# First maxima of a causal attention taken inside the feature loop; squares moved from GpSimd to ScalarE

## The reference

```python
q = split(x @ Wq); k = split(x @ Wk); v = split(x @ Wv)          # 16 heads of 16
q_amp = _amp_norm(q)      # a = softplus(t); a / sqrt(mean(a * a) + 1e-6), per head
k_amp = _amp_norm(k)
q_phi = pi * tanh(split(x @ Wqp)); k_phi = pi * tanh(split(x @ Wkp))
scores_dot = einsum(q, k) * scale
scores_phase = (einsum(q_amp*cos(q_phi), k_amp*cos(k_phi)) + einsum(q_amp*sin(q_phi), k_amp*sin(k_phi))) * scale
scores = scores_dot + lam * scores_phase
attn = softmax(where(causal, scores, -inf)); out = einsum(attn, v)
```

## Time and profile before

| | us |
|---|---|
| median of 3 runs | 1952.91 (1946.81 to 1959.45) |
| profiled execution, its time | 1948.98 |
| its span in the profile | 1947.3 |
| TensorE busy | 1737.1 (89% of the span) |
| DVE busy | 1262.3 (65%) |
| ACT busy | 882.6 (45%) |
| granted TensorE clock, mean | 0.941 |

### The profile page before, as it was taken

How to read it: one execution, slowest core, us unless ns; L and a number is a source line. 1 busy time by engine, 2 the same in 40 slices (tenths; PEclk the granted TensorE clock), 3 DMA queues, 4 the chain that set the end, 5 groups by cost and what they waited for, 6 DMA issues and landing times.

```text
span 1947.3 us, 28314 instructions
## 1 busy us (share of the span) xinstructions
PE 1737.1 (89%) x9130; PEld 920.4 (47%) x9131; DVE 1262.3 (65%) x2992; ACT 882.6 (45%) x1035; POOL 366.4 (19%) x478
## 2 busy tenths in 40 slices
PE   6998479999999999999999999977639999999965
PEld 3444234444444444444444444426525666666644
DVE  3677867777777777777777777516525555555536
ACT  2677524455555555555455554544311221221236
POOL 0111211111121111211211112103572111111111
PEclk9999768899999999999999999997759999999988
DMA  3366434011021020110201103016521111111144
GB/s 102 137 238 236 179 129 147 7 36 70 8 73 39 15 90 7 57 50 7 99 12 39 67 7 121 13 60 204 205 95 38 47 43 48 44 43 49 44 132 151
DMA packets 99497, 155.30 MB, mean 80 GB/s; under 512 B 10752, under 2 KB 60736, under 8 KB 99008
## 3 DMA queue, kind: packets, MB, share of 16 engines
q1 hardware_dynamic: 84928, 122.53, 18.9%
q0 software_dynamic: 14464, 31.40, 4.6%
HBM read 87.90 MB, written 65.35 MB: 79 GB/s over the span
## 4 chain that ended last, share of the span: by engine, by line
PE 70%; DVE 8%; ACT 7%; issue 6%; DMA 5%; POOL 2%; SPq 1%; another core or an unknown queue 0%; ACTq 0%; DVEq 0%; POOLq 0%
PE att_ps_s L884 22%; PE exp_ps_h L1564 13%; PE att_ps_o L903 12%; PE att_ps_m L862 10%; PE exp_ps_y L1582 6%; ACT att_probs L931 3%; DMA out_parts<-att_out_t 2%; PE pre_ps_q L311 2%; PE exp_ps_t L1572 2%; PE pre_ps_h L311 1%; DVE att_maxima L945 1%; DMA k_parts<-pre_waves 1%; PE exp_ps_x L1553 1%; POOL sorted_rows L1449 1%; DMA route_a_inv<-inv_rows 1%
## 5 line engine op out<-in xcount | busy, mean ns | idle before, releaser
L931 ACT ACTIVATE att_probs<-att_ps_s 128x1024 f32<-128x1024 f32 (+3 forms) x640 | 563.7, 895 | 484.4 <-PE att_ps_s L884 476.5
L884 PE MATMUL att_ps_s<-att_queries,att_keys 49*128 49x512 f32 (+3 forms) x2560 | 632.8, 561 | 20.9 <-ACT att_probs L931 11.4
L945 DVE TENSOR_REDUCE att_maxima<-att_ps_m 128x1 f32<-128x512 f32 x768 | 487.1, 684 | 153.6 <-PE att_ps_m L862 148.6
L862 PE MATMUL att_ps_m<-att_keys,att_queries 48*128 48x512 f32 (+3 forms) x1280 | 506.5, 605 | 24.1 <-DVE att_maxima L948 15.9
L862 PEld LDWEIGHTS att_ps_m<-att_keys,att_queries 48*128 48x128 f32 x1280 | 197.7, 193 | 315.8 <-DVE att_maxima L945 141.4
L884 PEld LDWEIGHTS att_ps_s<-att_queries,att_keys 49*128 49x128 f32 x2560 | 242.9, 191 | 127.3 <-ACT att_probs L931 85.4
L948 DVE CUSTOM_DVE_ANT_0 att_ps_m<-att_ps_m,att_future 128x128 f32<-128x128 f32 (+3 forms) x512 | 240.3, 514 | 73.4 <-PE att_ps_m L862 72.1
L903 PE MATMUL att_ps_o<-att_probs,att_values 128*32 128x512 f32 (+3 forms) x2560 | 269.3, 535 | 11.1 <-POOL att_probs L1034 11.1
L1564 PE MATMUL exp_ps_h<-keep_w,exp_rows_t 128*128 x568 | 257.4, 596 | 5.5 <-DVE exp_rows_t L1598 5.5
L1640 ACT ACTIVATE exp_hidden<-exp_product 128x512 f32<-128x512 f32 x71 | 44.8, 632 | 343.7 <-DVE exp_product L1623 343.7
L1034 POOL TENSOR_SCALAR_AFFINE_SELECT att_probs<-att_probs 128x512 f32<-128x512 f32 x128 | 81.1, 634 | 491.3 <-ACT att_probs L931 491.2
(11 more groups left out here) (179 smaller groups left out, 1458.6 us busy)
## 6 DMA issues: line engine op xcount, KB each, us to landing
att_queries<-q_parts SPq DMA_DIRECT2D x64, 192.0 KB
att_keys<-k_parts SPq DMA_DIRECT2D x64, 192.0 KB
exp_rows<-sorted_rows SPq DMA_DIRECT2D x71, 129.0 KB, 2.3
v_rows<-pre_v_sb SPq DMA_DIRECT2D x8, 1024.0 KB, 7.1
q_parts<-pre_waves SPq DMA_DIRECT2D x16, 512.0 KB, 4.2
k_parts<-pre_waves SPq DMA_DIRECT2D x16, 512.0 KB, 5.8
att_values<-v_rows SPq DMA_DIRECT2D x32, 256.0 KB
out_parts<-att_out_t POOLq DMA_DIRECT2D x32, 256.0 KB, 6.0
```

The lines of the kernel that those rows point to most:

```text
L862: pe.matmul(take()[:, 0:width], queries[g % 2][half, c, r, P * q:P * q + P], keys[g % 2][half, k, r, 0:width], start=True, stop=True).then ...
L884: mm = pe.matmul(score_tile(unit, first, last)[:, e], keys[g % 2][half, k // TPC, r, P * (k % TPC):P * (k % TPC) + P].bitcast(F32), querie ...
L931: act.activation(probs[:, step % PROBS, DUO * r:DUO * r + DUO, first:last], score_tile(unit, first, last), ACT.Exp, scale=SCALE).then_inc( ...
L945: dve.tensor_reduce(to, buf[:, 0:width], AX.X, ALU.max).then_inc(s_mr, 1)
```

## The change

Four things change.

1. The first 32 groups of maximum tiles of the first quad (64 tiles: chunk 0, chunk 1, and the first 8 of chunk 2's 24 groups) leave the attention. TensorE sends them inside the projections of chunks 4 to 7 (iterations 5 to 8), one group of two tiles after each half of a projection, so 8 groups an iteration; DVE takes them at 8 places of its iteration. They use a ring of two banks, so a send waits until DVE has read the tile two before.
2. The two banks come from `ps_n`, which is gone: `sum_norm` of Q now writes `ps_q`, and waits for the copy of the same iteration's K out of it (`s_qk`).
3. `square` is an ACT activation with lag 2, behind the tanh of Q, where it was a POOL multiplication with lag 1. On DVE the cosine `features` now stand ahead of the copy of K, where they stood behind it. TensorE's loop is written out.
4. The plan starts with 32 groups done and DVE and ACT busy until 8000 ns (`TAIL`). The ones under the second quad's keys are written by SP and no longer by POOL.

```diff
+EARLY_CHUNKS = range(NCH // 2, NCH)
+EARLY_TURNS = 8
+EARLY_GROUPS = len(EARLY_CHUNKS) * EARLY_TURNS
+    def send_early(self, pe):
+        for _ in range(DUO):
+            tile, self.sent = self.sent, self.sent + 1
+            if tile >= len(self.ring):
+                pe.wait_ge(self.s_mr, tile - len(self.ring) + 1)
+            self.send(pe, self.ring[tile % len(self.ring)], *self.early[tile])
...
-        ps_n = n.ps("ps_n", [P, 2, CH])
...
+            def project(i, weight, out, p, ready):
                 for c in range(2):
                     for k in range(DK):
                         mm = pe.matmul(...)
-                return mm
+                    if c == 1:
+                        mm.then_inc(ready, 1)
+                    if i in EARLY_CHUNKS:
+                        maxima.send_early(pe)
...
                 if side == Q:
                     pe.wait_ge(s_sq, i + 1)
+                    pe.wait_ge(s_qk, min(2 * i + 4, 2 * NCH))
...
+            def square(i, p):
+                act.wait_ge(s_amp, i + 1)
+                if since(i, 1):
+                    act.wait_ge(s_norm, 2 * i)
+                act.activation(amp_sq[:, :], amp[:, p], ACT.Square).then_inc(s_sq, 1)
...
             pipelined(act, NCH, [
                 (lambda i, p: phases(i, p, Q), 1),
+                (square, 2),
                 (lambda i, p: norm_exp(i, p) if i < NCH - 1 else None, 3),
...
             pipelined(dve, NCH, [
+                (take_early, 1),
                 (lambda i, p: keep_qk(i, p, Q), 1),
+                (take_early, 1),
                 (abs_phase, 2),
+                (take_early, 1),
                 (norm_amplitudes, 3),
+                (take_early, 1),
+                (lambda i, p: features(i, p, 0), 3),
+                (take_early, 1),
                 (lambda i, p: keep_qk(i, p, K), 1),
-                (lambda i, p: features(i, p, 0), 3),
+                (take_early, 1),
+                (take_early, 1),
+                (take_early, 1),
                 (keep_v, 1),
                 (amplitudes, 1),
                 (keep_x, 0),
                 (lambda i, p: features(i, p, 1), 3)])
...
-            def square(i, p):
-                pool.wait_ge(s_amp, i + 1)
-                if since(i, 1):
-                    pool.wait_ge(s_norm, 2 * i)
-                pool.tensor_tensor(amp_sq[:, :], amp[:, p], amp[:, p], ALU.mult).then_inc(s_sq, 1)
...
-        self.free = dict(pe=0, dve=0, act=0, pool=0)
+        self.free = dict(pe=0, dve=TAIL, act=TAIL, pool=0)
+        self.group = EARLY_GROUPS
```

More of the change, by code:

```diff
@@ L164, in absolute @@
     return dve.tensor_scalar(out.bitcast(U32), in_.bitcast(U32), 0x7FFFFFFF, None, ALU.bitwise_and)
-def prepare(nc, block, small, x, Wq, Wk, Wv, Wqp, Wkp, lambda_raw, q_parts, k_parts, v_rows, first_quad):
+BLOCKS = [TPC * (c + 1) for c in range(QC)]
+FIRST = [sum(BLOCKS[:c]) for c in range(QC)]
+STEPS = sum(BLOCKS)
+QUADS = B * NQ
+CHUNKS = QUADS * QC
+QUAD_LOADS = 16 * (2 * DUO + 1)
+MAX_TILES = [DUO * DUO * TPC * (c + 1) for c in range(QC)]
+SLOTS_PS = 3
+SLOTS_S = 2
+PROBS = 6
+BATCH = 2
+AHEAD = 3
@@ new lines, with chunk_of, own_block, hidden_columns @@
+SUMS = QUAD * CH // P
+SWITCH, SEEN, PLACED, SETTLED, EAGER, TAIL = 200, 200, 2200, 6000, 300, 8000
+def chunk_of(s):
+    return max(c for c in range(QC) if FIRST[c] <= s)
+def own_block(s):
+    c = chunk_of(s)
+    return s - FIRST[c] - TPC * c
+def hidden_columns(s):
+    return P * max(0, own_block(s))
+def ends_chunk(s):
+    return s + 1 in FIRST[1:] + [STEPS]
+def units_of(s):
+    return [(r, hidden_columns(s), CH) for r in range(DUO)]
+UNITS = [(s, *unit) for s in range(STEPS) for unit in units_of(s)]
@@ L321, in project_qk @@
                     pe.wait_ge(s_qk, 2 * i + side)
-                project(side, ps_q, p).then_inc(s_qkp, 1)
+                if side == Q and since(i, 2):
+                    pe.wait_ge(s_ln, 2 * i - 3)
+                project(i, side, ps_q, p, s_qkp)
             def project_phase(i, p, side):
@@ L364, in _ @@
                 (lambda i, p: sum_norm(i, p, K), 2),
-                (turn, 0)])
+                (turn, 0)], unrolled=True)
         @block.scalar
@@ L814, in attend, with put_ones @@
         vacated = {"max": s_mr, "turn_max": s_row}
-        CONSTS = 1
-        LOADS = 16 * (2 * DUO + 1)
+        def put_ones(eng, i):
+            eng.wait_ge(s_made, 1)
+            for e in range(DUO):
+                row = HALF * e + FEAT
+                eng.dma_start(keys[i][row:row + 1].rearrange("p c r t -> p (c r t)").bitcast(F32),
+                              ones[0:QC * DUO * CH // (P // 2)]).then_inc(s_one[i], 16)
         def chunk_row(g, c):
@@ L913, in _ @@
                 elif event == "max":
-                    max_tile(*what)
+                    highest.send(pe, take(), *what)
                 elif event == "turn_max":
@@ L977, in invert @@
                 dve.reciprocal(inverse[:, n % 2], sums[:, n % 2]).then_inc(s_inv, 1)
-            tile = 0
+            tile = DUO * EARLY_GROUPS
             for event, *what in plan:
                 if event == "max":
-                    take_max(*what, tile, ps_m[slots.pop(0)[0]])
+                    highest.take(dve, ps_m[slots.pop(0)[0]], tile, *what)
                     tile += 1
-                    if tile == sum(MAX_TILES[m % QC] for m in range(what[0] + 1)):
-                        negate(what[0], tile)
                 elif event == "turn_max":
```

187 lines of the change are left out of this document (90 added, 97 removed).

## The result

The changed kernel takes **1967.6 us** (median of 11 runs, 1961.5 to 1973.79) against 1952.91 (11 runs, 1946.81 to 1959.76): a ratio of **1.0069**, 95% interval 1.0049 to 1.0089. It is 0.7% slower, which is inside the 1% that the prediction called no change, and the interval lies wholly above 1.

The account below looks back on a forecast made before the run. The loop was taken to be bound by a ring through TensorE, ACT and DVE, the early attention by TensorE's waits and low clock. 8.8 + 46.6 + 2 - 45.5 = +12 gave 1965 us on the median; range 1934 to 1992.

Parts of the forecast that it names:

- case (a): The forecast itself: loop +57, attention -45 us; -5 to +28 with the bounds; chance 0.55.
- The ring: Loop's circle through TensorE, ACT and DVE: square and cosine features lengthen 23.9 to 28.3 us; iterations 3 and 4 +8.8.
- The lockstep: Iterations 5 to 8: sends and takes wait for each other through two banks; 36.1 us each, +46.6 in all.
- The tail: Loop's end: the last square on ACT waits behind `make_waves` and delays the path to the last features, +2 us.
- The start of the attention: Last features to first scores: 6.0 us instead of 14.64, the row being turned already, -8.6.
- To chunk 3: First scores to those of chunk 3: 82 us against 115.7, clock over 0.9, -33.8.
- the -3: At chunk 3's first scores: the slow start of a unit after a wait goes, an estimated -3 us.
- own bound of -12: Attention's smallest gain: only the 64 tiles' own 0.2 us each, all stalls come back; forecast -45.5.
- (b): Rival, loop: the lockstep isn't paid, only square and features lengthen the ring; -19, 1934 us; chance 0.16.
- (c): Rival, attention: stalls come back, scores wait for placed rows or maxima, only some 15 us gained; 1996 us; chance 0.12.
- (d): Rival, loop: TensorE stays at the lower clock from send 5 to V, +5 us an iteration; 1985 us; chance 0.17.
- Part 1: Loop's ring: square and features lengthen it by 4.4 us; DVE's 2.5 us back from POOL's contention don't show.

Follow-up runs that it names:

- e4: The changed kernel with V's projection ahead of the norm's sum of Q on TensorE: 1964.21 us, ratio 1.0067 to the kernel before.
- e1: The changed kernel with DVE's cosine features behind the eighth take, no longer ahead of K's copy: 1960.62 us, ratio 1.0042 to the kernel before.
- e5: The changed kernel with ACT's square ahead of the tanh of Q instead of behind it: 1954.07 us, ratio 1.0003 to the kernel before.
- e7: The changed kernel with the edits of e5 and e6 together: 1921.75 us, ratio 0.9842 to the kernel before.
- e6: The changed kernel with takes 4 and 5 ahead of `norm_amplitudes`, take 6 between it and K's copy, cosine features last: 1933.69 us, ratio 0.991.
- e8: The changed kernel with the square back on POOL at lag 1: 1958.46 us, ratio 1.0041 to the kernel before.
- e2: The changed kernel with DVE's takes 4 and 5 ahead of `norm_amplitudes`: 1960.7 us, ratio 1.0053 to the kernel before.
- e9: The e7 kernel with no maximum tile in the loop, all back in the attention: 1957.55 us, ratio 1.002 to the kernel before.

## Why the prediction was right

1965 was forecast and 1967.6 measured, by the mechanism of case (a): loop +66.4 (+57.4 forecast), from the last features on -51.7 (-45.5). The terms of the loop were 9 us too small, those of the attention 6 us, so most of the error cancelled in the sum. That the total came within 3 us is luck to that extent, the more since 4.8 of the attention's 51.7 us stand in "the rest", where single executions differ by more.

- **The ring, iterations 3 and 4: +8.8 forecast, +12.7 measured.** Right was the ring: e4's iteration 3, in which ACT's log does come last, is its 28.3 (28.31), and Square measured 1.90 where 1.9 was taken. e1 and e5 each take one of its two parts away, and both together (e7) give back 23.93. Wrong was the sentence that the norm's sum of Q "isn't later than the ring". It counted 1.8 and 3.5 us for sum and V. The wait for K's copy makes a gap of 3.94 us, and behind it they take 3.75 and 4.46, 2.7 us more in all, so that V and not ACT's log came last. The same rows' slow start was booked for iterations 5 to 8 and not here, where the gap was nearly as long.
- **The lockstep, iterations 5 to 8: 36.1 forecast for each, 36.7 to 37.4 measured.** The steps fell within a few tenths up to send 5: tanh of Q at 9.3 us after the start (8.65 forecast), normed amplitudes from 14.0 (13.4), send 5 at 16.7 (16.9) after 5.21 us of idle time (5.5). Mis-sized was the slow start behind it, booked at 1.0: K's second half took 3.44 us for 1.98 and the pair ahead of it 1.17 for 0.5, together 2.1, and DVE's K copy then waited for TensorE. That is the missing 1 us an iteration; with 35.1 (no slow starts) the error of an iteration would have been twice as large. The Trainium skill, "TensorE: Matmul & The Clock Gate", section "Why this matters for your kernels", which the prediction named, advises against idle gaps between bursts of matmuls. The trace agrees with it at the gaps of 5.21 us, and also at those of 3.94 us in iterations 3 and 4, where the prediction booked no slow start.
- **The tail, +2:** 2.2 measured. The norm's sum waits 8.12 us for ACT's square at 280.85, where it waited 7.44 for POOL's.
- **The start of the attention, -8.6:** -9.5. The row was placed 5.1 us after the last features, with 6.0 forecast.
- **To chunk 3, -33.8 and then -3:** -37.4 and -4.8. 82 us were forecast and 78.3 measured at the clock that was asked for ("over 0.9": 0.93). The estimate of 4.5 for a low clock at the start was about right: the first 10 us, 306.61 to 316.60, have a granted clock of 0.50, with TensorE busy for 9.65 us, and at twice the clock an estimated half of that would have done, so it cost some 4.8. The 3.7 us too many lie in the steps, further tiles or short forms, and which of them it is stays open. For the -3, no slow unit stands at 384.86 (1.88 for 8 records, where 4 took 2.08 at 365.54), an estimated 1 us from these two rows; the rest of the -3 is not shown, as said at the account. The attention's own bound of -12 would have made +45 of the sum, outside the "-5 to +28" of case (a).

Of the rivals, (b) (the lockstep isn't paid, 1934) isn't what this order gives, but e6 comes close to that case: iterations of 30.4 and 1933.69 us. It named the condition, iterations under 31, and what stands against it, the takes between normed amplitudes and K's copy, which is what e6 moves. The equal totals are chance: (b) kept the features in the ring and took 28.3 us for each iteration, and e6 has 25.73 and 27.42 for 3 and 4 and 30.4 to 31.7 for 5 to 7. (c) fell with 78.3 us at 0.93, and (d), slow from send 5 to V, with V's 3.62 at 192.73: the clock was back at 185.35, 7 us earlier. That none of POOL's contention with DVE would show, as Part 1 has it, is right for iterations 3 and 4 and wrong for those with tiles: there e8 pays 2.1 to 2.4 us an iteration for it.

Two things stay open. e6's 34 us are split into idle time and slow matmuls by the windows, but no run keeps the one without the other. A shorter gap alone didn't spare the slow start: behind e5's 3.41 us half a projection still took 3.24. And take 6's own place wasn't tried apart from takes 4 and 5.

## What to carry to other kernels

In a software pipeline with in-order engines, place each added instruction by when its operands are there, rather than by what it belongs to: behind an instruction that waits it hands that wait on to whoever waits for it, here a two-bank ring that passed ACT's exp through DVE's take on to TensorE. Take such edits together when they close one circle of waits (at most 7 us each alone, 34 together with one more take moved), and look for a place where the engine sits idle ahead of a wait whose end doesn't depend on it (the square ahead of tanh: 13.5 us for two exchanged lines). Work moved out of a starved stage can be a true gain (25 to 36 us here) inside a change that loses; undo the parts one by one before giving up the whole.

## What the runs showed of the hardware

- **How gaps and slow starts went together.** After TensorE's gaps of 3.94, 5.21 and 8.12 us the next matmuls ran at the lower of the two clock levels (1.2 instead of 2.4 GHz) at first: 3.75 for 1.88, 3.44 for 1.98, 3.78 for 1.88 us. Behind e5's 3.41 us it was 3.24 for 1.98. After 1.35 us alone (e1) and after 2.17 us in the loop before they didn't, after 2.14 us in e5 they did in part (2.95 for 1.88), and after 2.38 us in e1, with 1.35 us of idle time ten us ahead of it, they did (5.40 for 3.70). So the length of one gap doesn't tell it by itself.
- **A slow start moves with the gap.** e2 and e4 each removed a slow start from where it was and got it back elsewhere, at 1.8 and 2.7 us. It was gone (clock 1.00) where the iteration's other path was shortened so far that one gap of 1.6 to 2.2 us an iteration was left, ahead of Q's projection: e6's iterations 6 and 7, e7, and e9.
- **Square on ACT** took 1.90 us for 128 x 2048, as exp of the same size, without a table load between tanh and exp. In e7, between the waves and the load for tanh, it took 1.89 and added no load either.
- **Two 128x512 products of DVE beside POOL's 128x2048 multiplication** took 3.86 us (e8, and 3.87 before) where they take 1.41 without it. It cost nothing where DVE would have waited for TensorE anyway, and over 2 us an iteration where a take stood behind it (e8, iterations 6 and 7).
